# Attention with experts on one core: a product of two small one-hot matrices in the routing, and a mask moved ahead of a rope

## The reference

```python
top_vals, top_idx = jax.lax.top_k(gate_logits, 2)
w = jax.nn.softmax(top_vals, axis=-1)
y_all = jnp.einsum('td,eod->teo', xf, expert_w) + expert_b[None, :, :]
out = jnp.sum(jnp.take_along_axis(y_all, top_idx[:, :, None], axis=1) * w[:, :, None], axis=1)
```

## Time and profile before

| | |
|---|---|
| runs, median of 3 | 1007.92 us (1005.15 to 1008.72) |
| profiled execution, its own time | 1008.12 us |
| span from its first to its last instruction | 1006.3 us |
| mean granted TensorE clock | 0.982 of full speed |
| busy: TensorE / VectorE / ScalarE / GpSimd | 932.0 / 743.2 / 435.2 / 565.7 us |

### The profile page before, as it was taken

One profiled execution on the slowest core, in us unless ns is written; L12 is line 12 of the kernel. 1 busy time (PEld: TensorE's weight loads), 2 busy tenths in 40 slices (PEclk: granted clock), 3 DMA queues, 4 the chain that ended last, 5 costly groups with the idle time before them and its releaser, 6 DMA issues.

```text
span 1006.3 us, 18752 instructions
## 1 busy us (share of the span) xinstructions
PE 932.0 (93%) x6589; PEld 447.7 (44%) x6589; DVE 743.2 (74%) x1322; ACT 435.2 (43%) x711; POOL 565.7 (56%) x557
## 2 busy tenths in 40 slices
PE   2899989989999978988999999989999999999887
PEld 1344434434444433444555555544444444444333
DVE  7888988888889899543444444477878888788865
ACT  5367866666765432331211211214433444334442
POOL 1545675664676548572333333237887788777651
PEclk9999999999999999998999999999999999999999
DMA  6366588788785352385555555554555554455431
GB/s 238 106 220 223 146 278 311 204 300 292 206 291 209 117 210 85 134 309 177 179 168 176 179 170 174 168 214 142 184 159 176 191 191 148 148 181 179 157 107 54
DMA packets 107964, 188.63 MB, mean 187 GB/s; under 512 B 11873, under 2 KB 65249, under 8 KB 102625
## 3 DMA queue, kind: packets, MB, share of 16 engines
q1 hardware_dynamic: 97072, 152.03, 44.5%
q0 software_dynamic: 10800, 35.40, 12.3%
HBM read 117.13 MB, written 70.25 MB: 186 GB/s over the span
## 4 chain that ended last, share of the span: by engine, by line
PE 67%; DVE 12%; DMA 7%; POOL 6%; ACT 4%; issue 3%; SPq 1%; another core or an unknown queue 0%; DVEq 0%; ACTq 0%; POOLq 0%
PE psum L942 18%; PE psum L1027 11%; PE psum L1036 6%; PE psum L1051 6%; PE psum L990 6%; PE psum L977 5%; PE psum L959 5%; PE psum L993 5%; DMA x_in<-x 3%; PE psum L919 3%; DVE top L1463 3%; PE psum L961 2%; POOL gT L571 1%; DMA c_rows<-c_turn 1%; POOL y_in L616 1%
## 5 line engine op out<-in xcount | busy, mean ns | idle before, releaser
L756 ACT ACTIVATE pT<-psum,factors 128x512 f32<-128x512 f32 (+1 forms) x352 | 219.6, 640 | 267.6 <-PE psum L977 239.3
L1463 DVE TENSOR_REDUCE top<-psum 128x1 f32<-128x384 f32 (+3 forms) x352 | 210.7, 635 | 24.1 <-PE psum L961 23.1
L1027 PE MATMUL psum<-xT,w_att 128*128 128x512 f16 x768 | 199.0, 385 | 6.9 <-DVE xT L1414 4.8
L942 PE MATMUL psum<-w_exp,x_gT 128*128 x852 | 197.4, 382 | 0.8 <-DVE x_gT L1419 0.6
L959 PE MATMUL psum<-k_stack,q_stack 96*128 96x384 f16 (+3 forms) x512 | 129.1, 305 | 22.2 <-DVE top L1463 21.4
L606 POOL DMA_INDIRECT x_g<-xn_rows,tok_of x71 | 67.3, 948 | 143.8 <-PE psum L919 136.4
L977 PE MATMUL psum<-q_stack,k_stack 98*128 98x256 f16 (+3 forms) x512 | 129.5, 306 | 6.3 <-ACT pT L756 5.0
L1419 DVE TENSOR_TENSOR x_gT<-psum,x_gT 128x512 f16<-128x512 f32 x71 | 49.0, 692 | 106.9 <-ACT x_gT L780 94.4
L942 PEld LDWEIGHTS psum<-w_exp,x_gT 128*128 128x128 f16 x852 | 83.9, 98 | 87.4 <-issue 3.9
L780 ACT ACTIVATE x_gT<-psum 128x512 f16<-128x512 f32 x71 | 42.3, 597 | 173.2 <-PE psum L919 173.1
L590 POOL TENSOR_SCALAR_AFFINE_SELECT pT<-pT 128x512 f32<-128x512 f32 x128 | 99.3, 785 | 18.7 <-ACT pT L756 18.7
(11 more groups left out here) (172 smaller groups left out, 1283.9 us busy)
## 6 DMA issues: line engine op xcount, KB each, us to landing
y_rows<-y_sb SPq DMA_DIRECT2D x71, 256.0 KB
w_in<-w_all SPq DMA_DIRECT2D x12, 1024.0 KB, 9.6
q_stack<-qk_rows SPq DMA_DIRECT2D x96, 128.0 KB
k_stack<-qk_rows SPq DMA_DIRECT2D x96, 128.0 KB
x_in<-x SPq DMA_DIRECT2D x8, 1024.0 KB, 13.5
qk_rows<-q_hl SPq DMA_DIRECT2D x32, 256.0 KB, 2.2
qk_rows<-k_hl SPq DMA_DIRECT2D x32, 256.0 KB
xn_rows<-x_in SPq DMA_DIRECT2D x8, 1024.0 KB, 4.7
```

Of the source, the lines that this page charges most:

```text
L756: act.activation(p_of(j, h, heads), banks[BANK_T + (NT_ * n + k) % 2][:, 0:W], ACT.Exp, scale=factors[:, 0:1]).then_inc(exp_done, 1)
L942: now = pe.matmul(banks[s % 4], x_gT[s % 4][:, xp * C + c, :], w_exp[:, bass.ds(e, 1), wp, c, :].rearrange("p e d -> p (e d)"), start=n == ...
L1027: now = pe.matmul(bank, w_att[:, what, wp, c, g * P:(g + 1) * P], xT[b % 2][:, xp * C + c, :], start=at_pass == 0, stop=at_pass == 3 * C - 1)
L1463: return dve.tensor_reduce(out=top[:, h:h + heads, i], in_=banks[BANK_S + k % 2][:, 0:heads * W].rearrange("p (h t) -> p h t", h=heads), a ...
```

## The change

It does three things. The one-hot matrix of the tiles is not compared as a whole any more: the tile number is cut into its eighth (up to 9 of them) and its rest (0 to 7), two small one-hot matrices are compared, the one of the eighths is multiplied by the token numbers, and the big matrix is the product of the two, all on VectorE; GpSimd's four multiplications are gone. The routing operations stand at other places: the small matrices ahead of the normalisation in step 13, both products and one `spread_low` at the end of step 13, one `spread_low` ahead of the normalisation and two at the end of step 14, and `experts_of_tiles` at the end of step 15. Since its scratch now lies in the place of the eighth expert's weights, these are loaded behind it, in step 15 after `move_c`. And in every step with a k to be roped (0 to 28), GpSimd's mask 1 stands ahead of k's rope.

```diff
     at_low = at("at_low", [P, 2, NT, P], F16)
-    at_high = at("at_high", [P, 2, NT, NTILE], F16)
+    at_high = at("at_high", [P, 2, NT, NEIGHTS, 8], F16)
+    at_eight = at("at_eight", [P, 2, NT, NEIGHTS], F16)
+    at_rest = at("at_rest", [P, 2, NT, 8], F16)
+    past = at("past", [P, NTILE, E], F32)
+    n_past = at("n_past", [P, NTILE], F32)
...
                     load_exp(1)
-                    sp.wait_ge(exp_of_done, 1)
                     sp.wait_ge(parts_done, 1)
                     load_exp(2)
...
                     sp.wait_ge(tok_summed, 1)
-                    for e in range(4, E):
+                    for e in range(4, E - 1):
                         load_exp(e)
...
                 move_c(n + 1)
+                if n == CHOOSE + 4:
+                    sp.wait_ge(exp_of_done, 1)
+                    load_exp(E - 1)
                 store_qk(1, n + 3)
...
                 mask(n, 0)
                 if n + 3 < N:
                     low_qk(0, n + 3)
+                mask(n, 1)
+                if n + 3 < N:
                     rope(1, n + 3)
-                mask(n, 1)
                 if n >= N1 and n + 1 < N:
                     gather_y(late_tiles(n + 1)[1])
...
-                if n == CHOOSE + 2:
-                    for k in range(2):
-                        value_high(k, 0)
-                        value_high(k, 1)
...
                 own.link(dve.tensor_scalar(low_i[:], slots[:], P - 1, None, ALU.bitwise_and))
-                own.link(dve.tensor_scalar(high_i[:], slots[:], 7, None, ALU.logical_shift_right))
-                own.link(dve.tensor_copy(low16[:], low_i[:]))
-                dve.tensor_copy(high16[:], high_i[:]).then_inc(parts_done, 1)
+                dve.tensor_scalar(high_i[:, 0], slots[:], 10, None, ALU.logical_shift_right)
+                own.link(dve.tensor_scalar(high_i[:, 1], slots[:], 7, 7, ALU.logical_shift_right, ALU.bitwise_and))
+                dve.tensor_copy(low16[:], low_i[:])
+                dve.tensor_copy(high_parts[:], high_i[:]).then_inc(parts_done, 1)
...
+            def spread_high_parts():
+                dve.wait_ge(parts_done, 1)
+                dve.wait_ge(gate_done, B)
+                dve.wait_ge(xT_stored, 16 * (B - 2))
+                for place_no, (to, size) in enumerate(((at_eight, NEIGHTS), (at_rest, 8))):
+                    shape = [P, 2 * NT, size]
+                    now = dve.tensor_tensor(to[:].rearrange("p k t r -> p (k t) r"), count16[:, 0:size].unsqueeze(1).broadcast_to(shape),
+                                            high_parts[:, place_no].rearrange("p k t -> p (k t)").unsqueeze(2).broadcast_to(shape), ALU.is_equal)
+                own.link(now)
+                for k in range(2):
+                    now = dve.tensor_tensor(at_eight[:, k], at_eight[:, k], token16[:].unsqueeze(2).broadcast_to([P, NT, NEIGHTS]), ALU.mult)
+                own.link(now)
+
             def spread_high(k):
-                shape = [P, NT, NTILE]
-                dve.tensor_tensor(at_high[:, k, :, :], count16[:, 0:NTILE].unsqueeze(1).broadcast_to(shape),
-                                  high16[:, k, :].unsqueeze(2).broadcast_to(shape), ALU.is_equal).then_inc(at_high_done, 1)
+                shape = [P, NT, NEIGHTS, 8]
+                dve.tensor_tensor(at_high[:, k], at_eight[:, k].unsqueeze(3).broadcast_to(shape), at_rest[:, k].unsqueeze(2).broadcast_to(shape),
+                                  ALU.mult).then_inc(at_high_done, 1)
...
-                if n == CHOOSE + 3:
-                    spread_low(1, 0)
+                if n == CHOOSE + 2:
+                    spread_high_parts()
+                elif n == CHOOSE + 3:
+                    spread_low(0, 1)
                 if n and n != N1:
                     normalise_o(n - 1)
...
-                if n == CHOOSE + 2:
-                    dve.wait_ge(gate_done, B)
-                    dve.wait_ge(xT_stored, 16 * (B - 2))
-                    spread_high(0)
...
                     place_slots()
-                    experts_of_tiles()
                 elif n == CHOOSE + 2:
+                    spread_high(0)
                     spread_high(1)
                     spread_low(0, 0)
-                    spread_low(0, 1)
                 elif n == CHOOSE + 3:
+                    spread_low(1, 0)
                     spread_low(1, 1)
+                elif n == CHOOSE + 4:
+                    experts_of_tiles()
```

More of the change, by code:

```diff
@@ L46, in moe_attention_layer @@
     NTILE = (2 * T + E * (P - 1)) // P
+    NEIGHTS = (NTILE + 7) // 8
     HG = 4
@@ L91, in moe_attention_layer @@
     token16 = at("token16", [P, NT], F16)
+    high_parts = at("high_parts", [P, 2, 2, NT], F16)
     slots = at("slots", [P, 2, NT], I32)
@@ L117, in moe_attention_layer @@
     low16 = at("low16", [P, 2, NT], F16)
-    high16 = at("high16", [P, 2, NT], F16)
     cnt_i = at("cnt_i", [P, E], I32)
@@ L178, in moe_attention_layer @@
     low_i = at("low_i", [P, 2, NT], I32, place[0] - 4 * E * NT)
-    high_i = at("high_i", [P, 2, NT], I32, place[0] - 4 * E * NT + 8 * NT)
+    high_i = at("high_i", [P, 2, 2, NT], I32, place[0] - 4 * E * NT + 8 * NT)
     one_hot = [at(f"one_hot{k}", [P, NT, E], F32) for k in range(2)]
@@ L183, in moe_attention_layer @@
     picked = at("picked", [P, 2, NT, E], F32)
-    past = at("past", [P, NTILE, E], F32, slot[2])
-    n_past = at("n_past", [P, NTILE], F32, slot[2] + 4 * E * NTILE)
     assert place[0] <= slot[3]
@@ L221, in moe_attention_layer @@
     gap_done, gap_exp, w12_done, exp_of_done = (sem(n) for n in ("gap_done", "gap_exp", "w12_done", "exp_of_done"))
-    parts_done, at_low_done, at_high_done, at_high_valued = (sem(n) for n in ("parts_done", "at_low_done", "at_high_done", "at_high_valued"))
+    parts_done, at_low_done, at_high_done = (sem(n) for n in ("parts_done", "at_low_done", "at_high_done"))
     tok_summed, tok_done, bias_loaded = sem("tok_summed"), sem("tok_done"), sem("bias_loaded")
@@ L571, in low_x @@
                 pool.tensor_tensor(by_blocks(gT[:, C + k, :]), x_blk[b % 2][:, :, k * HD:(k + 1) * HD], by_blocks(gT[:, k, :]), ALU.subtract).then_inc(x_lo_done, 1)
-            def value_high(k, h):
-                here = at_high[:, k, h * NT // 2:(h + 1) * NT // 2, :]
-                pool.wait_ge(at_high_done, k + 1)
-                pool.tensor_tensor(here, here, token16[:, h * NT // 2:(h + 1) * NT // 2].unsqueeze(2).broadcast_to([P, NT // 2, NTILE]),
-                                   ALU.mult).then_inc(at_high_valued, 1)
             def rope(what, m):
@@ L909, in tokens_of_slots @@
                 pe.wait_ge(at_low_done, 4)
-                pe.wait_ge(at_high_valued, 4)
+                pe.wait_ge(at_high_done, 2)
                 for k in range(2):
                     for t in range(NT):
-                        now = pe.matmul(banks[BANK_QV][:, 0:NTILE], at_low[:, k, t, :], at_high[:, k, t, :],
+                        now = pe.matmul(banks[BANK_QV][:, 0:NTILE], at_low[:, k, t, :],
+                                        at_high[:, k, t, :, :].rearrange("p a r -> p (a r)")[:, 0:NTILE],
                                         start=k + t == 0, stop=k * NT + t == 2 * NT - 1)
```

1 line of the change is left out of this document (removed).

## The result

| | before | after |
|---|---|---|
| median of the runs | 1006.53 us (1002.35 to 1008.72) | 1024.63 us (1021.38 to 1025.22) |
| ratio, 95% interval | | 1.0176 (1.0147 to 1.0205) |
| profiled execution, its span | 1008.12, 1006.3 us | 1021.38, 1019.6 us |

The changed kernel is slower by 18.1 us; 1017.5 was forecast, with 1000 to 1028 as the range. The profiled execution of after is the fastest of its runs, so the traces account for 13.3 of the 18.1 us. A few runs of other kernels that took some 90 us longer, at a granted clock of 0.85, are left out of all medians and ratios.

A forecast was written before the change was run, and what follows sets the result against it. TensorE, busy 93% of the span, was taken as the bound. Routing -9.6, steps 0 to 11 +14, steps 17 to 28 +4 and experts +1 gave +9.4 on 1008.1: 1017.5 us, range 1000 to 1028.

The forecast's parts named there:

- (1) to (3): Routing in steps 12 to 14: three TensorE waits of 0.8, 1.4, 1.5 left, half clock gone; gains 2.1, 2.9, 4.6 us.
- The 1.3 us set against it: Step 13, small matrices: time by the skill's table instead of 2.3 us, which would end them 1 us earlier.
- (4): Ends of steps 13 and 14: VectorE's products hidden under TensorE's work; nothing, or up to 1 us in step 14.
- (5): Steps 0 to 11: mask makes rope and copy of k late, colliding with `low_w`; +14 us, bounds -7 and 22.
- the first rival: Whole kernel: only the routing counts, late rope stays under TensorE's work; 999.5 us, chance 0.14.
- The routing terms: Routing work in steps 12 to 14, lowered clock counted: together 9.6 us gained, bounds 6 and 13.
- The even rival: Whole kernel: no collisions, each rope 1.2 late in about eight tight steps; about 1008.5 us, chance 0.17.
- SP "is nothing": SP's queue: longer wait for k's low half, store and stacks later, costs nothing since scores need them two steps later.
- (6): Steps 17 to 28: GpSimd's later work shifts by 1.1 us, 0.3 lost a step at the third mask; +4 us.
- (7): Start of the experts: late gathered rows and eighth expert's weights, mostly swallowed by the fifth gather's wait; +1 us (-2 to +4).

The follow-up runs named there:

- e1: The changed kernel with k's rope ahead of the second mask again, so the routing alone; 1002.85 us, ratio 0.9967 to the kernel before.
- e5: The changed kernel with mask 1 ahead of k's rope only in steps 13 and 14; 999.32 us, ratio 0.9911 to the kernel before.
- e10: e6 with SP's store of k and the stacks' loads moved into the next step, behind weights and x; 1006.36 us, ratio 1.0009.
- e7: The changed kernel with VectorE's `low_w` waiting until GpSimd has finished k's rope; 1024.37 us, ratio 1.0145 to the kernel before.
- e6: The changed kernel with ScalarE's copy of k and GpSimd's low half of k at the step's end in steps 0 to 10; 1041.02 us, ratio 1.0333.
- e9: e5 with small matrices at step 13's end and the first `at_low` operation in four pieces in step 14; 995.41 us, ratio 0.9902.
- e12: e9 with three of the four `at_low` pieces as one operation at the end of step 14; 1000.30 us, ratio 0.9934.
- e2: The kernel before with the second mask ahead of k's rope as the only edit; 1031.14 us, ratio 1.0242.

## Why the prediction was right in direction and short in size

**(1) to (3), routing: right, -9.6 forecast, -10.5 measured** in steps 13 to 15. The three waits came within 0.4 us of their forecasts, and the granted clock was 1.00 behind them. The price of the small matrices was right too: 0.75 + 0.69 + 0.83 = 2.27 us on VectorE for 2.3. The 1.3 us set against it were not the page's rule after all: the Trainium skill's "VectorE: DVE Perf Modes", section "What auto-detection actually checks", wants 16 bits and a step of 1 or -1 in every tensor for the faster mode, and one operand of each of these operations repeats its elements along the row. For the slower mode the Trainium skill's "VectorE: DVE Perf Modes", section "The perf-mode tier table", has 2.29 us for 2048 elements, which agrees with the 2.28 of the earlier trace rows.

**(4), "Nothing" for the end of step 13: wrong, hidden by the other part of the change.** It looked at VectorE's cover alone. The price of VectorE's and GpSimd's two-input operations taking turns, which (5) uses, was not applied here. In e1 it costs 2.56 and 2.02 us of waits; in the changed kernel the mask ahead of the rope avoids them (e5). So it is in part luck that the routing's sum fits: by itself the routing gave 4.0 us in these steps (e1), and the mask, forecast only to cost, gave 6.5 more. And the first rival, the routing alone at 999.5 us, is 1002.85 in e1.

**(5), steps 0 to 11: +14 forecast, +21.5 measured; the mechanism right, the term mis-sized.** The copy of k is 3.5 late in step 2 for a forecast of 3.4, and e10 shows that the work queued behind this copy and behind GpSimd's low half carries 17.7 of the 21.5. Three things were off:
- *The lowered clock was left out.* In steps 1 to 12 TensorE's idle time grew from 19.4 to 34.0 us, by 14.5, which is the forecast; its busy time, for the same products, grew from 257.4 to 264.4, by 7.0, with a mean clock of 0.97 for 1.00. The routing terms had counted just this; (5) did not, and it is the size of the whole error. (Some of it comes and goes: e5, with the old order in these steps, has 261.6 us busy at 0.98.) In e10 the clock is 1.00 again; compared with after, 10.9 us of the idle and 6.8 of the busy time are gone. In after the clock fell behind waits of 3.61, 4.49, 2.59, 2.92 and 2.93 us, to 0.67, 0.50, 0.57, 0.59 and 0.60 over some 4 us each; behind one of 2.89 at 313.49 us it stayed at 1.00. First steps 1 to 12 as one stretch, in before, after and e10; then TensorE and the stretches of after, beside those shown above:

```profile
74.60:351.44 276.84, 257.41 (x2161) 121.00 (x2153) 237.86 (x490) 185.58 (x287) 172.21 (x158) 1.00 0.72 234
74.52:372.90 298.38, 264.42 (x2149) 124.29 (x2153) 229.25 (x490) 186.82 (x287) 176.90 (x157) 0.97 0.65 217
74.87:355.53 280.66, 257.59 (x2161) 120.94 (x2153) 234.24 (x490) 186.29 (x287) 177.14 (x157) 1.00 0.70 231
...
109.12 0.29 PE L892 MATMUL psum<-ident,amax 128*128 128x128 f32 x1 [3.61 <-ACT w_abs L718]
...
161.43 1.04 PE L987 MATMUL psum<-pT,v_sb 128*32 128x256 f32 x8 [2.59 <-POOL pT L589]
...
212.35 0.29 PE L892 MATMUL psum<-ident,amax 128*128 128x128 f32 x1 [2.92 <-ACT w_abs L718]
...
287.27 0.29 PE L892 MATMUL psum<-ident,amax 128*128 128x128 f32 x1 [2.93 <-ACT w_abs L718]
...
109.00:113.00 4.00, 3.88 (x38) 1.94 (x39) 2.92 (x9) 1.96 (x2) 0.00 (x0) 0.67 0.93 240
...
161.00:165.00 4.00, 3.44 (x57) 1.87 (x58) 2.70 (x7) 2.37 (x3) 3.20 (x4) 0.57 0.87 228
...
212.00:216.00 4.00, 3.65 (x62) 2.39 (x63) 1.59 (x6) 0.21 (x2) 1.95 (x3) 0.59 1.01 242
287.00:291.00 4.00, 3.73 (x66) 2.47 (x67) 1.82 (x7) 0.12 (x2) 1.87 (x3) 0.60 0.90 230
```

- *Where it falls.* Behind steps 0 to 10 the next step took 0.0, 3.75, 4.65, 2.2, 1.1, 3.5, 0.0, -1.5, 4.2, 2.4 and 1.2 us more than before, for 0.5, 2.4, 2.4, 2.4, 0.5, 2.4, 1, 0.5, 1, 2.4 and 0. (The -1.5 is not the mask's: e1 has -1.3 there.) The steps differ from the forecast both ways, so it is luck in part that the idle time comes to the forecast's 14.
- *What waits.* TensorE's waits for low x were to grow past 2 us; they fell from 2.3 us in all to 0.6, since the magnitudes, which it needs first, now come later than low x. And waits for masks did not give 1.5 back in these steps: they went from 1.8 to 2.6 us, since one of 2.59 came (at 161.43) in place of three short ones.

The even rival, "no collisions", fell in the trace of after: the copy of k is 1.2 us late only in steps 0, 4 and 7, without `low_w`, and 2.4 to 4.2 in the others up to 10. e7 keeps `low_w` out of the rope, and the loss is the same, only behind another engine.

**SP "is nothing": right for this change, wrong as a rule.** In the changed kernel SP itself waits 113.2 us for k's low half, 64.7 before, but no engine waits longer for weights or x (VectorE's row statistics 11.4 us in all, 11.9 before). In e6, with k's store later still, SP's queue behind it cost more than everything else.

**(6), steps 17 to 28: +4 forecast, +3.7 measured.** One such stretch of after:

```profile
749.00:770.00 21.00, 20.82 (x156) 9.57 (x156) 15.37 (x29) 8.99 (x16) 15.74 (x17) 1.00 0.51 156
```

TensorE lacks 0.18 of 21 us, once a step, ahead of the third mask's products; 0.3 was forecast. So the plain steps lost less than forecast, some 2 us in all; one step that lost 1.2 and step 17 with 0.6 make up the 3.7, by luck.

**(7), start of the experts: +1 forecast, -0.8 measured,** within the 6 us over which that stage varies here. TensorE now waits 3.97 us ahead of the first tile, in place of before's wait for the fifth gather. SP's issue of the eighth expert's weights in after, their time to landing, and the first product with the experts' weights:

```profile
451.93 0.34 SPq L372 DMA_DIRECT2D w_exp<-w_rows  x1
...
w_exp<-w_rows SPq DMA_DIRECT2D x1, 1024.0 KB, 5.3
...
458.62 0.61 PE L939 MATMUL psum<-w_exp,x_gT 128*128 x1 [3.97 <-issue]
```

The weights land at 457.20, and the product starts 1.4 us behind that, as it does in all twelve kernels here that load them in step 15 behind `move_c`. So the wait is for these weights. The length of the stage follows when they land, counted from the end of step 15: 9.9 us in e1 (stage 240.21), 10.4 in e9 (240.53), 12.6 in after (243.35), 13.9 in e5 (244.10), 16.2 in e12 (246.49). Most of that is the time of the issue, which SP comes to 4.7 us behind the step's end in e1 and e9, 7.4 in after, 8.4 in e5 and 10.8 in e12. The forecast saw this load as the risk, but took the wait for the fifth gather to swallow most of it.

What stays open: the 4.8 us between the traces' difference (13.3) and the medians' (18.1), and what makes SP come to the eighth expert's weights sooner or later, at which no experiment was aimed.

## What to carry to other kernels

A small operation that waits late should not be put ahead of work that others queue behind: 0.6 us of mask cost 24 (e2), by its 2 us of waiting at the head of GpSimd's queue and three queues behind it (ScalarE's, GpSimd's own, and SP's when pushed further). Price TensorE's waits together with the lowered clock that follows them in the trace, and in every stage alike. And test the parts of a change one by one and step by step: this one held a gain of 9 us (e5), part of which needed the very reordering that lost some 25 elsewhere.

## What was not expected of the hardware

How much VectorE's two-input operations and GpSimd's operations in SBUF stretch each other when both come back to back: GpSimd's mask, 0.63 us alone, took 2.95, a rope operation of 1.27 took 3.55, and VectorE's piece of 0.68 took 1.11 to 1.65, which is its own time and much of GpSimd's operation. Cut into pieces, VectorE's work took 4.20 us there, about twice three pieces of 0.68. The Trainium skill's "SBUF — State Buffer", section "Who interferes with whom", has this as an exclusive lock of the two engines' shared port pair; these rows agree. What they add is that two such streams side by side alternate operation by operation, so that the engine with the shorter ones loses most.
